# Graph layers on one core: two penalty tiles in one ScalarE instruction, normalisation sums from accumulators, and new slot tables

## What is computed

```python
# x: 8 x 2048 x 128, adj: 8 x 2048 x 2048, fp32
x = layernorm(x + L0(x, adj))
x = layernorm(x + L1(x, adj))

# L0, in blocks of 64 rows: Wh = x @ W; e = leaky(Wh @ a, 0.2)
scores = softmax(adj_block * e); out = scores @ Wh
z = leaky(leaky(out @ W1 + b1) @ W2 + b2) @ W3 + b3 + out
L0 = normalised z * ln_g + ln_b

# L1, 4 heads of 32: h = x @ W_proj.T
scores = leaky(s_left[i] + s_right[j] + adj * we, 0.2)
scores += NEG * (adj <= 1e-5)          # the penalty
out = leaky(x + softmax(scores) @ h + bias, 0.5)
```

## Time and profile before

| | |
|---|---|
| median of three runs | 1992.19 us (1987.78 to 1993.39) |
| the profiled execution | 1992.15 us |
| its span, first to last instruction | 1990.3 us |
| busy: GpSimd, VectorE | 1863.7 us (94%), 1865.5 us (94%) |
| busy: TensorE, ScalarE | 1804.3 us (91%), 1547.9 us (78%) |
| mean granted TensorE clock | 0.981 |

### The profile page before, as it was taken

The page is one execution under the profiler, slowest core; times in us unless marked ns, Lnnn a source line. Parts: engine busy times, 40 slices in busy tenths (PEclk is TensorE's granted clock), DMA queues, the critical chain, the costliest instruction groups (busy, mean ns, idle before and its releaser), DMA issues.

```text
span 1990.3 us, 34086 instructions
## 1 busy us (share of the span) xinstructions
PE 1804.3 (91%) x11080; PEld 883.8 (44%) x11080; DVE 1865.5 (94%) x3557; ACT 1547.9 (78%) x3415; POOL 1863.7 (94%) x663
## 2 busy tenths in 40 slices
PE   7799998999989998999989998999998999888885
PEld 6544444444444444445444444444444444333332
DVE  3699999999999998999989999899999999999997
ACT  6678887898778887788878888788887897666664
POOL 3599999999999999999999999999999999999996
PEclk8899999999999999999999999999999999999999
DMA  3233324233243243333233332333324233233310
GB/s 100 73 112 94 101 70 134 85 119 100 68 118 112 85 120 99 93 101 109 80 99 119 86 110 87 99 115 95 101 70 129 90 112 91 89 109 91 109 51 11
DMA packets 138088, 190.61 MB, mean 96 GB/s; under 512 B 22328, under 2 KB 56504, under 8 KB 137912
## 3 DMA queue, kind: packets, MB, share of 16 engines
q1 hardware_dynamic: 137912, 188.44, 32.0%
HBM read 179.77 MB, written 8.65 MB: 95 GB/s over the span
## 4 chain that ended last, share of the span: by engine, by line
DVE 43%; PE 23%; issue 18%; POOL 12%; ACT 2%; SPq 0%; DVEq 0%; DMA 0%; ACTq 0%; POOLq 0%
DVE X L1110 30%; PE psum L1229 19%; POOL X L499 11%; DVE X L1099 5%; PE psum L1408 4%; DVE st L936 1%; DVE x1s L993 1%; POOL haug L482 1%; DVE res L1053 1%; DVE est L936 1%; DVE psum L1044 1%; DVE lky L1059 1%; ACT o_sb L662 1%; DVE mv L942 1%; ACT E L765 0%
## 5 line engine op out<-in xcount | busy, mean ns | idle before, releaser
L499 POOL TENSOR_TENSOR X<-RHO,E 128x1536 f32<-128x1536 f32 (+1 forms) x512 | 1776.4, 3504 | 55.9 <-ACT E L765 51.2
L1110 DVE SCALAR_TENSOR_TENSOR X<-psum,s_j,X 128x512 f32<-128x512 f32 x2048 | 1397.7, 738 | 49.4 <-POOL X L499 44.7
L1229 PE MATMUL psum<-X,haug 128*33 128x512 f32 x4096 | 991.3, 605 | 3.1 <-DVE X L1110 3.1
L765 ACT ACTIVATE E<-psum,we_s 128x512 f32<-128x512 f32 x512 | 396.9, 775 | 264.4 <-PE psum L1229 263.1
L1408 PEld LDWEIGHTS psum<-ident,adj_sb 128*128 128x128 f32 x2048 | 287.8, 141 | 589.7 <-DVE X L1110 442.4
L1408 PE MATMUL psum<-ident,adj_sb 128*128 128x128 f32 x2048 | 434.1, 293 | 123.5 <-DVE X L1110 120.9
L1229 PEld LDWEIGHTS psum<-X,haug 128*33 128x33 f32 x4096 | 196.4, 111 | 429.9 <-issue 393.7
L768 ACT ACTIVATE psum<-psum,we_s 128x512 f32<-128x512 f32 x512 | 380.9, 744 | 0.0
L1229 PE MATMUL psum<-sgn_ident,pen 128*128 128x128 bf16 x2048 | 377.5, 221 | 0.0
L726 ACT ACTIVATE pen<-adj_sb,pen_bias 128x512 bf16<-128x512 f32 x512 | 367.2, 717 | 0.4
L1099 DVE TENSOR_TENSOR X<-psum,E 128x512 f32<-128x512 f32 x496 | 333.5, 672 | 4.7 <-ACT psum L561 2.3
(11 more groups left out here) (227 smaller groups left out, 1446.7 us busy)
## 6 DMA issues: line engine op xcount, KB each, us to landing
adj_sb<-in_adj_dram SPq DMA_DIRECT2D x128, 1024.0 KB, 5.2
RHO<-rho_scratch SPq DMA_DIRECT2D x31, 1024.0 KB, 9.8
out_dram<-o_sb SPq DMA_DIRECT2D x32, 256.0 KB, 2.9
xg<-in_x_dram SPq DMA_DIRECT2D x28, 256.0 KB, 5.6
blk<-in_adj_dram SPq DMA_DIRECT2D x56, 64.0 KB, 5.3
X<-in_x_dram SPq DMA_DIRECT2D x2, 256.0 KB, 3.0
W_sb<-in_L_gnn_W_dram SPq DMA_DIRECT2D x4, 64.0 KB, 1.9
X<-in_adj_dram SPq DMA_DIRECT2D x4, 64.0 KB, 2.8
```

The lines of the kernel that those rows point to most:

```text
L499: Q.tensor_tensor(X[m % NX][:, 0:heads, :], RHO[:, g % 2, 0:heads, :], bc(E[m % NE][:], 1, [P, heads, GROUP]), ALU.mult).then_inc(B_pool, 1)
L765: A.activation(E[m % NE][:], TA[m % NT], ACT.Exp, scale=we_s[:, 3:4], bias=we_s[:, 5:6]).then_inc(E_sb, 1)
L1110: ins = V.scalar_tensor_tensor(slot[:, h, :], TA[m % NT], s[:, k, h:h + 1], slot[:, h, :], ALU.mult, ALU.max)
L1229: return T.matmul(o, l, r, start=start, stop=stop)
```

## The change

Three edits. First, `penalty` writes two tiles with one instruction of 128x1024, in every even slot, and nothing in odd ones; the eight buffers of one tile become four of two. Secondly, the means come from accumulator outputs of the instructions that write r and lky (for lky, four instructions of 128x128 in place of one of 128x512), and the variances from squares that ScalarE takes with the negated mean as its bias, with an accumulator output too; `bn_stats` and `bn_aggr` stay only in the first batch's start (`first_moments`, `first_var`). Thirdly, the tables are new. Most steps move by none to two slots; `x1T`, `g0` and the like follow, `FOUR` goes from (7, 35) to (11, 29).

```diff
-    FOUR = (7, 35)
+    FOUR = (11, 29)
...
-          "oT": (-7, 13, 24, 35), "y1": (-6, 14, 25, 36), "y2": (-5, 15, 26, 36), "ssq": (-2, 17, 28, 39),
-          "z_rstd": (-2, 19, 28, 40), "r_rstd": (4, 22, 35, 44), "r_norm": (6, 25, 38, 48), "x1T": (8, 29, 45, 50),
+          "oT": (-7, 13, 24, 34), "y1": (-6, 14, 25, 35), "y2": (-5, 14, 27, 36), "ssq": (-2, 17, 28, 39),
+          "z_rstd": (0, 19, 28, 39), "r_rstd": (3, 22, 37, 44), "r_norm": (6, 24, 40, 49), "x1T": (7, 29, 46, 50),
...
-    AT_DVE = {"max": (-20, -9, 10, 25), "rin": (-16, -8, 13, 27), "res": (0, 19, 30, 41), "r_stats": (2, 20, 33, 42)}
+    AT_DVE = {"max": (-20, -13, 12, 26), "rin": (-18, -6, 16, 27), "res": (1, 19, 30, 42)}
...
-    EPI_PE = {"back0": 1, "back1": 3}
+    EPI_PE = {"back0": 2, "back1": 3}
...
-    EPI_DVE = {"part0": 3, "part1": 5, "stats": 7}
-    EPI_POOL = {"shift": 12}
+    EPI_DVE = {"part0": 4, "part1": 5, "lky": 6}
+    EPI_POOL = {"shift": 15}
...
-        pen = [sb(f"pen{r}", [P, GT, P], bf16) for r in range(NPEN)]
+        pen = [sb(f"pen{r}", [P, GT, 2 * P], bf16) for r in range(NPEN // 2)]
...
-            def invstd(log, out, minus, mean_var):
-
-                A.activation(log, mean_var[:, :, 1], ACT.Ln, bias=eps_c[:])
-                link(copy(minus, mean_var[:, :, 0], -1.0))
+            def invstd(log, out, minus, sums, sq, src):
+
+
+                link(copy(minus, sums, -1.0 / D))
+                for t in range(GT):
+                    ins = A.activation(squares[:, t, :], src(t), ACT.Square, bias=minus[:, t:t + 1],
+                                       accum_out=sq[:, t:t + 1])
+                link(ins)
+                link(A.activation(log, sq, ACT.Ln, scale=1.0 / D, bias=eps_c[:]))
                 return A.activation(out, log, ACT.Exp, scale=-0.5)
...
-                if m >= MT:
+                if m >= MT or m % 2 == 1:
                     return
                 act.wait_ge(adj_in[c], 16 * (g + 1))
                 if m >= NPEN:
-                    act.wait_ge(adjT_ps, m - NPEN + 1)
-                A.activation(pen[m % NPEN][:], adj_sb[c][:, :, (k % CHUNK) * P:(k % CHUNK + 1) * P],
+                    act.wait_ge(adjT_ps, m - NPEN + 2)
+                A.activation(pen[m // 2 % (NPEN // 2)][:], adj_sb[c][:, :, (k % CHUNK) * P:(k % CHUNK + 2) * P],
                              ACT.Relu, scale=-BIG, bias=pen_bias[:]).then_inc(pen_sb, 1)
...
                     ins = V.scalar_tensor_tensor(x1_of(c)[:, t, :], mid_bank(c)[:, tsl(t)], rstd[s][:, t:t + 1],
-                                                 xb[s][:, t, :], ALU.mult, ALU.add)
+                                                 xb[s][:, t, :], ALU.mult, ALU.add,
+                                                 accum_out=rsum[s][:, t:t + 1])
...
-                V.tensor_tensor(lky[:], BK_B.rearrange("p (t f) -> p t f", t=GT), x1_of(g)[:], ALU.add).then_inc(lky_sb, 1)
...
+                for t in range(GT):
+                    ins = V.scalar_tensor_tensor(lky[:, t, :], BK_B[:, tsl(t)], 1.0, x1_of(g)[:, t, :], ALU.mult, ALU.add,
+                                                 accum_out=esum[:, t:t + 1])
+                ins.then_inc(lky_sb, 1)
```

More of the change, by code:

```diff
@@ L135, in build_program @@
         lky = sb("lky", [P, GT, D])
-        est6 = sb("est6", [P, GT, 6])
-        emv = sb("emv", [P, GT, 2])
+        esum = sb("esum", [P, GT])
+        esq = sb("esq", [P, GT])
+        squares = sb("squares", [P, GT, D])
         elog = sb("elog", [P, GT])
@@ L187, in build_program @@
         ssq = [sb(f"ssq{v}", [P, GT]) for v in range(6)]
-        st6 = [sb(f"st6{v}", [P, GT, 6]) for v in range(6)]
-        mv = [sb(f"mv{v}", [P, GT, 2]) for v in range(6)]
+        first_st = [sb(f"first_st{c}", [P, GT, 6]) for c in U]
+        first_mv = [sb(f"first_mv{c}", [P, GT, 2]) for c in U]
+        rsum = [sb(f"rsum{v}", [P, GT]) for v in range(6)]
+        rsq = [sb(f"rsq{v}", [P, GT]) for v in range(6)]
         lg = [sb(f"lg{v}", [P, GT]) for v in range(6)]
@@ L752, in epi_rstd @@
             def epi_rstd(g):
-                act.wait_ge(evar, GT * (g + 1))
-                invstd(elog[:], erstd[:], enmu[:], emv).then_inc(erstd_sb, 1)
+                act.wait_ge(lky_sb, g + 1)
+                invstd(elog[:], erstd[:], enmu[:], esum[:], esq[:], lambda t: lky[:, t, :]).then_inc(erstd_sb, 1)
             def epi_norm(g):
@@ L932, in _ @@
             V = nc.vector
-            def moments(st, src, done):
-                for t in range(GT):
-                    ins = V.bn_stats(st[:, t, :], src(t))
-                ins.then_inc(done, 1)
-            def mean_var(st, out, ready, count, done):
-                dve.wait_ge(ready, count)
-                for t in range(GT):
-                    V.bn_aggr(out[:, t, :], st[:, t, :]).then_inc(done, 1)
             def first_logits(c):
@@ L961, in first_zn, with first_moments, first_var @@
                 ins.then_inc(zn_first, 1)
+            def first_moments(c):
+                wait_r(dve, c)
+                for t in range(GT):
+                    ins = V.bn_stats(first_st[c][:, t, :], x1_of(c)[:, t, :])
+                ins.then_inc(st_first, 1)
+            def first_var(c):
+                dve.wait_ge(st_first, c + 1)
+                for t in range(GT):
+                    V.bn_aggr(first_mv[c][:, t, :], first_st[c][:, t, :]).then_inc(var_first, 1)
             def first_norm(c):
                 s = set_of(c)
-                dve.wait_ge(rstd_r, c + 1)
+                dve.wait_ge(rstd_first, c + 1)
                 for t in range(GT):
-                    ins = V.tensor_scalar(x1_of(c)[:, t, :], x1_of(c)[:, t, :], mv[s][:, t, 0:1], rstd[s][:, t:t + 1],
+                    ins = V.tensor_scalar(x1_of(c)[:, t, :], x1_of(c)[:, t, :], first_mv[c][:, t, 0:1], rstd[s][:, t:t + 1],
                                           ALU.subtract, ALU.mult)
@@ L1079, in epilogue @@
                         (epi_rden, epi_scale, epi_add)[part](g - 1, r)
-                if k == EPI_DVE["stats"]:
-                    (epi_lky, epi_moments, epi_var)[part](g - 1)
+                if k == EPI_DVE["lky"] and part == 0:
+                    epi_lky(g - 1)
             def tile(m):
@@ L1132, in host @@
                             residual(c)
-                        if n == AT_DVE["r_stats"][u] and part < 2:
-                            (r_moments, r_var)[part](c)
                     if n == ONCE_DVE["rm"] and part == 0:
@@ L1408, in transposes @@
                     T.matmul(o, adj_sb[c][:, t, at:at + P], ident[:], is_transpose=True, start=True, stop=False)
[L1409 removed]
+                    ins = mm(o, pen[m // 2 % (NPEN // 2)][:, t, half2(m)], sgn_ident[:], start=False)
                 ins.then_inc(adjT_ps, 1)
```

82 lines of the change are left out of this document (32 added, 50 removed), and 6 rows, old and new, of the table AT_PE.

## The result

| | before | changed |
|---|---|---|
| median of 20 runs each, side by side | 1991.39 us (1987.25 to 1995.01) | 1988.38 us (1987.06 to 1989.72) |
| ratio to before, 95% interval | | 0.9985 (0.9979 to 0.9992) |
| profiled execution, its span | 1992.15, 1990.3 us | 1988.07, 1986.2 us |
| mean granted TensorE clock | 0.981 | 0.992 |

The change gains 3 us.

A forecast was written before the change was run, and what follows sets the result against it. GpSimd's work was taken as the floor, only its idle time to be won: 18.5 (batches 1 to 5) + 2.7 (batch 0) + 2.5 (batch 6) - 1.0 (end) = 22.7 us off 1992.15, so 1969 us, range 1949 to 1987.

The forecast's parts named there:

- The rival in which VectorE gets nothing back: Accumulator outputs at 0.28 us each give VectorE 1.0 us more a batch: 1980 to 1988 us, chance 0.15.
- the sign that was named: The forecast is wrong if GpSimd waits at 11, 27, 43 or 59, or VectorE for the prelu over a microsecond.
- a burst: ScalarE's new reciprocal deviation: negation, four squares, logarithm, exponential, 2.35 us together, 1.8 more than before, eight times a batch.
- 57 and 58: GpSimd's waits of 1.81 and 0.2 us at these slots go, since lky is written before tile 54: 2.0 us.
- 3 and 9: GpSimd's waits at these slots, 0.8 us, both go: residual no longer before tile 0, statistics gone from slot 2.
- the new wait at 23: Slot 22's burst makes E(23) 1.7 us late, a new wait of 0.6; with 22's 0.95 gone, net 0.35 less.
- the term of 0.35 us "for small waits I don't see": Taken off the summed 4.05 us of saved waits, leaving 3.7 for each of batches 1 to 5.
- The epilogue's stretch: ScalarE's epilogue burst at k = 10, an even slot too, makes 4.7 us between two E's.
- the third rival: Bursts on even slots pass through to GpSimd; at 0.9 us each some 2014 us, chance 0.10.
- the won 3.7: Waiting saved of GpSimd's 7.2 us in each of batches 1 to 5, 18.5 us in all.
- The last batch: GpSimd was taken to wait for next to nothing there, so no gain was credited.
- The end: After the last lky, the logarithm 1.2 us later and 0.2 less behind it: 1.0 us more.

The follow-up runs named there:

- the short burst: Changed kernel with each four squares replaced by one square and one copy of four columns, no accumulators, variance left out: 1969.82 us, ratio 0.9888.
- the split: Changed kernel with each burst cut in two, two squares in the slot and two with the logarithm in the next: 1983.20 us, ratio 0.9954.
- e8_pairs_odd: Changed kernel with the double penalties in ScalarE's odd slots, three tiles ahead in place of four: 1976.86 us, ratio 0.9923.
- e11_penalty_first: Changed kernel with the penalty moved ahead of the woven steps in ScalarE's loop: 2019.59 us, ratio 1.0143.
- e10_tables_only: Kernel before with the new tables alone, single penalties and statistics kept on VectorE: 2007.90 us, ratio 1.0079.

## Why the prediction was wrong, and where it was right

**What bounds the kernel: right.** GpSimd's busy time stayed (1863.7 to 1865.2 us), and in every kernel run the time followed its idle time.

**VectorE: right, its relief a little larger.** 6.2 us in the third batch and 5.5 a batch over the whole run, in place of 5.0. Groups by form of VectorE, after:

```profile
L1064 DVE SCALAR_TENSOR_TENSOR lky<-psum,x1s 128x128 f32<-128x128 f32 x128 | 29.6, 287 | 14.5 <-ACT psum L762 14.5
...
L1064 DVE DVE_READ_ACCUMULATOR lky<-psum,x1s 128x1 f32 x128 | 10.6, 83 | 0.0
```

An accumulator output is an instruction of its own: the trace has one read for each, of 83 ns, against the 94 that I took from bn_aggr. The Trainium skill says so too ("VectorE: DVE Perf Modes", section on two Vector instructions with no wait between them), and the trace agrees. The rival in which VectorE gets nothing back is out. The other half of that row is the sign that was named: lky waits for the prelu, 15 times and up to 1.5 us.

**ScalarE: right in the sizes of its steps.** Squares of 0.39 us, a burst of 2.36 (forecast 2.35), a pair of 1.144 (forecast 1.14), and E to E in slot 22 of 5.06 (forecast 5.0); in all 7.4 us more in the third batch, for 8.7. The Trainium skill ("ScalarE: Activation LUTs", section on what ACT_TABLE_LOAD costs) gives an instruction with a pointer for its bias 280 ns and 0.833 ns a column, which by estimate makes a square of 128 columns 387 ns. The trace agrees, with 391.

**The waits one by one: here it failed.** The waits that the step took away did go: 57 and 58, 3 and 9, 22, most of 37; TensorE's wait for lky (17.4 us before) is gone; and the new wait at 23 is 0.77 (forecast 0.6). Those at 19 and 53, which were to stay, went too, and 46 wholly. With 23 counted in, the places that the step looked at gave 5.0 us in the third batch, more than the 3.75 that its terms make there (2.0, 0.8, 0.35, 0.4 and 0.2). What failed is the term of 0.35 us "for small waits I don't see" and, with it, costing the bursts and pairs of all slots but 22 as hidden. In the third batch 4.1 us of waits are new, at 11, 15, 27, 29, 35, 38, 41, 43 and 45: 4.1 stands where the sum had 0.35. The epilogue's stretch was worked out as 4.7 us and measured 4.74, but its consequence was never drawn: at that place the slack ends at a stretch of 3.95. I had compared 5.0 "against 3.7 of a tile" in slot 22 and then asked of the other slots only whether VectorE's lag had fallen.

That makes it, in kind, the third rival, with 0.10 far too unlikely. Its sizes were not right either. In the last batch 0.8 us of each burst reaches GpSimd, but in batches 1 to 5 the short burst gives back only 9.8 us in all, some 0.25 for each of the 40 bursts, where 0.45 was to use up the won 3.7. So in full batches the squares took about half of the gain, and the rest was lost at other slots, or was not there to win. The runs put sizes on it: the squares beyond the short burst cost 18.5 us where I had 4 (0.6 a batch), and the pair's place 11.5 where I had 0.4 at slot 37 and inside slot 22's sum, and otherwise a saving that cost nothing. Of the 18.6 us between the 22.7 forecast and the 4.1 by which the profiled executions differ, the squares are thus some 14; that the short burst lands at 1969.82, the forecast, is luck: it has some 4.3 us of waits in a full batch, where the forecast left 3.5.

**The last batch: wrong.** "Waits for next to nothing" (1.1 us) held for the kernel before; but the four epilogue bursts, with the double penalties behind them, stand in this batch too, and are its 3.3 us.

**The end: wrong in size.** 0.3 us longer in place of 1.0.

**Still open.** How much of the 18.5 us is the length of single stretches, and how much that ScalarE is later at the steps TensorE takes: the split returned 5, and in full batches slots 11, 15, 35 and 51 keep their waits (0.82, 0.45, 0.81, 0.63) even with short bursts. At 11 the double penalty then stands behind a step that itself waits for TensorE. Odd pairs remove all four, but bring 3.1 us at 8, 16, 36 and 50 for these 2.7, so at these places the parity only moves the waits; what it gains, it gains behind bursts, as its being worth nothing with short bursts says too. No run varied the places in the tables for odd pairs, which slots 8 and 50 of `e8_pairs_odd` ask for, had odd pairs in the old tables, or short bursts with single penalties. Why the penalty first costs 26 to 31 us in the changed kernels is argued from the waits of TensorE and VectorE, not shown. And no run separates the tables from the granted clock: it is 0.979 to 0.982 in the kernels with the old tables and 0.985 to 0.993 in those with the new ones, but for 0.979 in `e11_penalty_first`. Within the new tables it does not set the times apart: 0.989 goes with 1976.86 us (`e8_pairs_odd`) and with 2007.90 (`e10_tables_only`).

## What to carry to other kernels

Where a feeding engine runs in order, price its work by the longest stretch between two of its products on which the bottleneck waits, slot by slot, and not by its busy sum: here 44 idle microseconds in 238 did not hide a stretch that was 0.8 too long. How long it may be differs from place to place (3.95 and 4.29 us here), so read it from the waits of each. Merging two instructions saved 0.17 us a pair here (5.4 us in 32), but put 0.43 more in front of the next product (1.144 in place of 0.717); put the merged one where nothing else stands (one number, `LEAD = 3`, was worth 11.5 us). And read the bottleneck's idle time first: with its work fixed, the time of 20 kernels was this idle time and 1933 to 1938 us; what caused it had to be found elsewhere.

## What the runs showed beyond what was expected

- At these places one microsecond too many on ScalarE is one on GpSimd: 4.74 and 4.31 us from E to E gave waits of 0.79 and 0.36, and 3.70, where odd pairs take the 1.04 of the penalty out, gave none. In slot 22 it was 5.06, 4.63 and 4.06 us, with waits of 0.77, 0.34 and none.
- Gains and losses did not add across tables: the same sums were +35 us in one set and -25 in another, while pair and sums added up in the old tables (11 and 35 against 45).
- GpSimd's product stayed at 3.50 to 3.52 us in all kernels, whatever VectorE had to do beside it.
